# Projection with halves of heads as row tiles; values' bias later, sine products from PSUM, scale inside the exponential

## The reference

```
q, k, v = heads(x @ Wq.T + bq), heads(x @ Wk.T + bk), heads(x @ Wv.T + bv)
q, k = rope(q), rope(k)        # Y*cos + concat(-Y[8:], Y[:8])*sin
att  = softmax(where(causal, q @ k.T / 4, -inf));  y = (att @ v) @ Wo.T + bo
x    = layernorm(x + y)
h    = silu(x@w1.T*s1) * (x@w2.T*s2);  h = gelu(h@h1.T*hs1);  h = gelu(h@h2.T*hs2)
out  = layernorm(x + h@w3.T*s3)
```

## Time and profile before

| | us |
|---|---|
| median of three runs | 2792.42 (2791.34 to 2792.55) |
| the profiled execution's own time | 2795.36 |
| its span, first to last instruction | 2793.6 |
| projection stage, up to the first work of attention | 133.7 |
| all that follows | 2659.9 |

### The profile page before, as it was taken

How to read it: one execution, slowest core, us unless ns; L and a number is a source line. 1 busy time by engine, 2 the same in 40 slices (tenths; PEclk the granted TensorE clock), 3 DMA queues, 4 the chain that set the end, 5 groups by cost and what they waited for, 6 DMA issues and landing times.

```text
span 2793.6 us, 39368 instructions
## 1 busy us (share of the span) xinstructions
PE 2729.1 (98%) x14880; PEld 1424.9 (51%) x14880; DVE 1899.9 (68%) x4003; ACT 1348.4 (48%) x2641; POOL 138.3 (5%) x206
## 2 busy tenths in 40 slices
PE   8899999999999999999999999999999999999998
PEld 4423333333333333333323333588888887888887
DVE  6999999888888888888887774633333352443343
ACT  4436666777776777777777776411111111000100
POOL 3300110001100001100000000000000000000000
PEclk9979999999999999999999999999999999999999
DMA  7731110001110011110001000411111132121100
GB/s 217 204 74 39 30 30 26 3 15 32 29 43 6 5 33 32 30 34 3 1 3 39 19 5 9 118 58 58 58 58 58 43 128 108 46 82 54 45 16 23
DMA packets 95613, 133.47 MB, mean 48 GB/s; under 512 B 31462, under 2 KB 69094, under 8 KB 91718
## 3 DMA queue, kind: packets, MB, share of 16 engines
q1 hardware_dynamic: 81452, 96.25, 10.7%
q0 software_dynamic: 6336, 23.34, 3.8%
q10 hardware_dynamic: 7648, 11.54, 1.5%
HBM read 83.77 MB, written 47.32 MB: 47 GB/s over the span
## 4 chain that ended last, share of the span: by engine, by line
PE 88%; DVE 6%; issue 2%; ACT 1%; DMA 1%; SPq 0%; ACTq 0%; POOLq 0%; POOL 0%; DVEq 0%
PE wi_f L984 19%; PE at_o L533 18%; PE at_row L498 17%; PE at_key L512 16%; PE na_h L1202 13%; PE na_y L1214 3%; DVE at_segmax L584 3%; DVE fr_masked L580 1%; DMA values<-pr_vals 1%; ACT at_probs L648 1%; PE at_key L515 1%; PE wi_p L833 1%; DVE pr_parts L252 0%; DVE pr_full L248 0%; PE pr_main L130 0%
## 5 line engine op out<-in xcount | busy, mean ns | idle before, releaser
L648 ACT ACTIVATE at_probs<-at_key 128x512 f32<-128x512 f32 (+3 forms) x2304 | 1127.3, 567 | 502.4 <-PE at_key L512 353.2
L584 DVE TENSOR_REDUCE at_segmax<-at_row 128x1 f32<-128x512 f32 x1792 | 1142.8, 684 | 169.2 <-PE at_row L498 164.9
L512 PE MATMUL at_key<-fr_q_stack,fr_k_stack 99*128 99x512 bf16 (+3 forms) x1152 | 415.0, 365 | 1.3 <-ACT at_probs L648 1.0
L498 PE MATMUL at_row<-fr_k_stack,fr_q_stack 96*128 96x512 bf16 (+3 forms) x1152 | 404.6, 376 | 10.8 <-DVE at_mask L612 5.5
L498 PE MATMUL at_row<-at_k_stack,at_q_stack 96*128 96x512 bf16 (+3 forms) x1152 | 408.1, 364 | 1.8 <-DVE at_segmax L584 1.1
L512 PE MATMUL at_key<-at_q_stack,at_k_stack 99*128 99x512 bf16 (+3 forms) x1152 | 402.2, 364 | 7.5 <-ACT at_probs L648 6.9
L1202 PE MATMUL na_h<-fr_h,fr_h2w_h 128*128 128x512 f32 x1024 | 322.1, 396 | 1.4 <-DVE fr_h L730 1.4
L533 PE MATMUL at_o<-at_probs,fr_values 128*32 128x512 f32 (+3 forms) x2304 | 289.0, 574 | 0.0
L533 PE MATMUL at_o<-at_probs,at_values 128*32 128x512 f32 (+3 forms) x2304 | 287.9, 572 | 0.0
L580 DVE CUSTOM_DVE_ANT_0 fr_masked<-at_row,fr_causal 128x384 f32<-128x384 f32 (+3 forms) x512 | 243.8, 483 | 45.1 <-PE at_row L498 44.7
L498 PEld LDWEIGHTS at_row<-fr_k_stack,fr_q_stack 96*128 96x128 bf16 x1152 | 110.3, 99 | 308.3 <-DVE at_segmax L584 160.1
(11 more groups left out here) (121 smaller groups left out, 2558.1 us busy)
## 6 DMA issues: line engine op xcount, KB each, us to landing
hidden<-wi_h SPq DMA_DIRECT2D x64, 256.0 KB, 2.0
na_h2f<-hidden SPq DMA_DIRECT2D x8, 1024.0 KB, 7.7
q_parts<-pr_parts SPq DMA_DIRECT2D x48, 128.0 KB, 2.4
k_parts<-pr_parts SPq DMA_DIRECT2D x48, 128.0 KB, 3.3
at_q_stack<-q_parts POOLq DMA_DIRECT2D x48, 128.0 KB, 3.5
at_k_stack<-k_parts POOLq DMA_DIRECT2D x48, 128.0 KB, 3.8
values<-pr_vals SPq DMA_DIRECT2D x32, 136.0 KB, 3.3
outputs<-at_outs SPq DMA_DIRECT2D x128, 34.0 KB
```

Of the source, the lines that this page charges most:

```text
L498: last = nc.tensor.matmul(bank[:, 0:w], qst[u][0:SROWS, c, h, i * P:(i + 1) * P], kst[u][0:SROWS, h, s * CH:s * CH + w], start=True, stop= ...
L512: last = nc.tensor.matmul(bank[:, q0:CH], kst[u][0:SROWS + PARTS, h, j * P:(j + 1) * P], qst[u][0:SROWS + PARTS, c, h, q0:CH], start=True, ...
L584: nc.vector.tensor_reduce(segmax[:, n % 2, h * TPC + i, s:s + 1], row_ps[r % RING_R][:, 0:w], op=ALU.max, axis=AX.X).then_inc(rows_taken, 1)
L648: nc.scalar.activation(probs[:, g % RING_P, h, q0:CH], key_ps[m % RING_K][:, q0:CH], ACT.Exp).then_inc(probs_ready, 1)
```

## The change

Within `project` two units become one *pair*: 16 pairs, q and k of each chunk. The rows of the weights are reordered on the host, so that tile 0 holds the first halves of all 16 heads and tile 1 the second halves (`halves`). Then the rotation is an exchange of the two tiles: `full` half 0 = t1[0] - t2[1], half 1 = t1[1] + t2[0]. PE's `rotate`, its banks and `turn` go. DVE's sine product reads main's PSUM bank itself and adds the bias in the same instruction (`scalar_tensor_tensor`). hi, mid, rest and the third part go over both halves at once (1024 columns). SP stores each half with its three parts in one transfer (384 KB). ACT, not DVE, takes the values out of PSUM, without a bias. The bias of the values, which commutes with the softmax's weighted mean, is added to the outputs in `Prepare.scale`. The scale 1/4 goes into the exponential. `load_first` moves from ACT's queue to SP's; PE's waits for the constants and for the values move to where they are first needed. `parts` has 3 slots of pairs instead of 4 of units.

The diff, cut to the core:

```diff
@@ project, scalar
+            def take_values(n, i):
+                if n == 0:
+                    act.wait_ge(v_ones, 1)
+                else:
+                    act.wait_ge(v_stored[i], 32 * n)
+                act.wait_ge(v_ready, 2 * n + i + 1)
+                nc.scalar.activation(vals[:, i, :, :, 0:HD], v_ps[i][:, :, :].rearrange("p j (h d) -> p j h d", d=HD), ACT.Copy
+                                     ).then_inc(v_taken, 1)
...
             for g in range(NU + 1):
                 if g + 1 < NU:
                     linear(g + 1)
                 if g < NU:
-                    act.wait_ge(full_ready, g + 1)
+                    take_values(*divmod(g, PAIRS))
+                    act.wait_ge(full_ready, 2 * g + 2)
                     if g >= SLOTS:
-                        act.wait_ge(parts_stored[g % SLOTS], 16 * PARTS * (g // SLOTS))
-                    nc.scalar.activation(parts[:, g % SLOTS, 0, :], full[:, g % 2, :], ACT.Copy).then_inc(hi_ready, 1)
+                        act.wait_ge(parts_stored[g % SLOTS], 16 * 2 * (g // SLOTS))
+                    nc.scalar.activation(parts[:, g % SLOTS, 0, :, :], full[:, g % 2, :, :], ACT.Copy).then_inc(hi_ready, 1)
...
-                if 2 <= n < 2 + FIRST_EARLY:
...
-                    front.load_first(act, qp_d, kp_d, n - 2, range(m, len(TERMS), UNITS))
@@ project, vector
-                    dve.wait_ge(rot_ready, g + 1)
-                    nc.vector.tensor_tensor(t2[:, g % 2, :], rot_ps[g % 2][:, :], sin[:, n % BUFS, :], ALU.mult
-                                            ).then_inc(t2_ready, 1)
+                    for half in range(2):
+                        dve.wait_ge(lin_ready, 2 * g + half + 1)
+                        if g >= 1:
+                            dve.wait_ge(full_ready, 2 * (g - 1) + 2 - half)
+                        nc.vector.scalar_tensor_tensor(out=t2[:, half, :], in0=main_ps[2 * (g % 2) + half][:, :],
+                                                       scalar=bias[:, 2 * m + half:2 * m + half + 1], in1=sin[:, n % BUFS, :],
+                                                       op0=ALU.add, op1=ALU.mult).then_inc(t2_ready, 1)
...
-                if g < NU and m % 2 == 1:
...
-                    if n > 0:
-                        dve.wait_ge(v_stored[i], 32 * n)
-                    for j in range(2):
-                        last = nc.vector.tensor_tensor(
-                            vals[:, i, j, :, 0:HD], v_ps[i][:, j, :].rearrange("p (h d) -> p h d", d=HD),
-                            bv[:, :].rearrange("p (h d) -> p h d", d=HD), ALU.add)
@@ project, sync
+                early = n - 2
+                if 0 <= early < FIRST_EARLY:
...
+                    front.load_first(sp, qp_d, kp_d, early, range(m, len(TERMS), PAIRS))
                 sp.wait_ge(parts_ready, g + 1)
-                for a in range(PARTS):
-                    sp.dma_start((qp_d, kp_d)[m // DH][a, (m % DH) * P:(m % DH + 1) * P, n, :], parts[:, g % SLOTS, a, :]
-                                 ).then_inc(parts_stored[g % SLOTS], 16)
...
+                for half in range(2):
+                    sp.dma_start((qp_d, kp_d)[m].rearrange("a (p f) n t -> f p a n t", f=2)[half, :, :, n, :],
+                                 parts[:, g % SLOTS, :, half, :]).then_inc(parts_stored[g % SLOTS], 16)
+                sp.wait_ge(v_taken, g + 1)
+                for j in range(2):
+                    sp.dma_start(v_d[:, :, n, 2 * m + j, :].rearrange("q p e -> p q e"),
+                                 vals[:, m, j, :, :].rearrange("p (q h) e -> p q (h e)", q=NQUAD)
+                                 ).then_inc(v_stored[m], 16)
@@ attend, scalar
-                    nc.scalar.activation(probs[:, g % RING_P, h, q0:CH], key_ps[m % RING_K][:, q0:CH], ACT.Exp
+                    nc.scalar.activation(probs[:, g % RING_P, h, q0:CH], key_ps[m % RING_K][:, q0:CH], ACT.Exp, scale=HD ** -0.5
@@ Prepare.scale
         for a in range(DH):
             self.nc.vector.tensor_tensor(o[:, n % 2, a, :], o[:, n % 2, a, :], self.front.recip[:, :], ALU.mult
+                                         ).then_inc(self.scaled, 1)
+        for a in range(DH):
+            dve.wait_ge(self.scaled, DH * n + a + 1)
+            self.nc.vector.tensor_scalar(o[:, n % 2, a, :], o[:, n % 2, a, :], self.front.bv[:, a:a + 1], None, ALU.add
                                          ).then_inc(self.y_ready, 1)
```

More of the change, by code:

```diff
@@ L119, in main @@
             def main(g):
-                n, m = divmod(g, UNITS)
+                n, m = divmod(g, PAIRS)
                 if m == 0:
                     pe.wait_ge(x_loaded[n % BUFS], 16 * (n // BUFS + 1))
[L124 to L141, removed]
+                if n == 0:
+                    pe.wait_ge(w_loaded[m], 16)
+                for half in range(2):
+                    if g >= 2:
+                        pe.wait_ge(lin_ready, 2 * (g - 2) + half + 1)
+                        pe.wait_ge(t2_ready, 2 * (g - 2) + half + 1)
+                    bank = main_ps[2 * (g % 2) + half]
+                    for c in range(DH):
+                        last = nc.tensor.matmul(bank[:, :], w[m][:, c, half * P:(half + 1) * P], xt[:, n % BUFS, c, :],
+                                                start=(c == 0), stop=(c == DH - 1))
+                    last.then_inc(main_ready, 1)
             def values(n, i):
@@ L153, in values @@
                 last.then_inc(v_ready, 1)
-            main(0)
             for g in range(NU):
[L157 to L161, removed]
+                main(g)
+                values(*divmod(g, PAIRS))
         @block.scalar
         def _(act):
[L165 to L169, removed]
-            def linear(g):
[L173 to L179, removed]
+            def linear(g):
+                m = g % PAIRS
+                for half in range(2):
+                    act.wait_ge(main_ready, 2 * g + half + 1)
+                    if g >= 2:
+                        act.wait_ge(t1_ready, 2 * (g - 2) + half + 1)
+                    nc.scalar.activation(lin[:, g % 2, half, :], main_ps[2 * (g % 2) + half][:, :], ACT.Identity,
+                                         bias=bias[:, 2 * m + half:2 * m + half + 1]).then_inc(lin_ready, 1)
+            def take_values(n, i):
+                if n == 0:
+                    act.wait_ge(v_ones, 1)
[4 more added lines that the diff above has]
+                                     ).then_inc(v_taken, 1)
             load_weight(act, 0, "WqT")
@@ L814, in spread @@
         if n > 0:
-            queue.wait_ge(self.y_ready, DH * n)
+            queue.wait_ge(self.scaled, DH * n)
         for e in range(self.COPIES):
```

136 lines of the change are left out of this document (63 added, 73 removed).

## The result

The changed kernel takes 2869.35 us (median of 4 runs, 2867.56 to 2870.09), the kernel before 2791.88 beside it (4 runs, 2790.97 to 2792.55): ratio 1.0277 [1.0259, 1.0295]. Forecast was 2866, range 2828 to 2892. The profiled execution took 2867.56, its span is 2865.7.

The account below looks back on a forecast made before the run. PE bounds the span (98% busy), DVE the projection's pairs. A new closed loop, 12 x 13.2 + 10.7 = 169 us, puts the first maximum at 208: +74 on the 2792.4 median gives 2866 us, range 2828 to 2892.

Parts of the forecast that it names:

- The loop: Projection: ACT's taking of values, ahead of `hi`, waits for the store of pair g-2; 13.2 us per pair, chance 0.60.
- Length of a turn: Projection, per pair: 7.2 us from `hi` to parts' end, 5.4 to the values' landing, 0.6 for taking them.
- The meeting of POOL and DVE: Projection: POOL's products hold up DVE's full and parts; a pair takes 13.2 us, 10.7 without the meeting.
- The store's term: Projection: from parts' end to the values' landing 5.4 us; last issue starts 1.4 behind, bounds 4.35 and 13.
- The estimate from the Trainium skill: Four transfers after the parts: about 2.0 us fixed plus bytes at 436 GB/s, landing some 4.4 us after them.
- The loads in five of twelve turns: ACT's three loads ahead of linear: POOL's meeting avoided, 2.5 us less, against about 2.8 us more; left at 13.2.
- Start and end: Projection: third `hi` at 33.5 us, last turn 10.7, last `hi` at 202.6, first maximum at 208; shift +74.
- What is hidden: Values' bias at most 11 us if exposed, taken as nothing; first loads on SP covered; wait for `parts_stored` nothing.
- The numbers I gave for single rows: Profile after: ACT waits 6 to 8 us for the values' DMA, 14 times; PE busy 83 of 208 us.
- the shorter loop: Rival: POOL and DVE miss each other or the landing hides extra bytes; 10.7 per pair, +44, 2836 us; chance 0.24.
- No change: Rival: no loop, but POOL always against DVE's operations with two SBUF inputs; 7.3 per pair, 2789 us; chance 0.04.
- faster: Rival: the store lands so early that `hi` never waits; 6.0 per pair, 2770 us; chance 0.05.

Follow-up runs that it names:

- 2: Changed kernel with four value buffers instead of two, every queue's order as it was: 2785.93 us, ratio 0.9975 to the kernel before.
- 1: Changed kernel with SP storing the values ahead of its wait for the parts: 2800.16 us, ratio 1.0029 to the kernel before.
- 3: Changed kernel with the values' two stores issued ahead of the parts' stores, still behind the wait for the parts: 2840.09 us.
- 4: Changed kernel with a pair's parts stored in six transfers of 128 KB instead of two of 384 KB: 2878.82 us.
- 5: Changed kernel with both products on DVE, none on POOL, and no linear tiles on ACT: 2840.37 us.
- 10: Kernel before, with ACT taking the values ahead of `hi` in place of DVE, values' bias left out: 2797.58 us, ratio 1.0016.
- 11: Changed kernel with DVE, not ACT, taking the values at the end of its iteration: 2868.43 us.
- 12: Changed kernel with DVE taking the values, and loads of x issued once the pair before has its values taken: 2846.07 us.
- 8: Changed kernel with four value buffers, four slots of `parts` and both products on DVE: 2775.86 us, ratio 0.9938 to the kernel before.
- 9: Changed kernel with four value buffers, four slots, both products on DVE, and the values' store ahead of the wait for parts: 2773.25 us, ratio 0.9934.

## Why the prediction was right, point by point

- **The loop** was read rightly: taking the values waits for a store that stands behind the parts of the pair two before. Shown by 2 (with more buffers the slowdown is gone), 1 (with the store issued earlier nearly so), 3 to 5 (each part of the turn shortened or lengthened moves the time by about thirteen times that).
- **What closes it** was told only in part. I laid the weight on ACT's order ("stands ahead of `hi`"). Runs 10 to 12 show that ACT's place is the smaller half: ACT ahead of `hi` in units costs 6 us at the first maximum, and DVE's own place in pairs costs 77 us (11), or 54 when the loads of x are out of the way (12). What closes the loop is that one iteration is now a pair: the store of two pairs ago is issued behind the parts of the very iteration in which the buffer is asked for. In the kernel before these parts were done two iterations of a unit earlier: the store is issued at 119.86, and DVE asks for the buffer at 125.09, 5.2 us later (I had called this a whole pair, 6.67).
- **Length of a turn:** 7.2 + 5.4 + 0.6 = 13.2 forecast, 6.7 + 6.35 + 0.5 = 13.56 at 102.5 us, 13.32 on average. Two errors cancel in part, and that 2866 came within 4 us of 2869 is to this extent luck.
  - The meeting of POOL and DVE was forecast at 2.5, run 5 gives 2.15.
  - The store's term was too small by 0.95 in this turn. The last issue starts 1.76 behind the parts' end (110.98) where I had 1.4, since the values' two issues take 1.83 us behind 384 KB transfers and not 1.06; from there to the landing 4.6 passed where I took 4.0.
  - The estimate from the Trainium skill (DMA: Bandwidth & Descriptors, Anatomy of one DMA) of 4.4 from the parts is farther off; the measured 6.35, or 5.8 in the calmer turn, decides.
  - Half a us of the landing goes with something that I overlooked: the loads of the stacks, issued right behind the values' stores (from 112.15 on). In the eight landings without them the last issue's start is followed by the landing after 4.0 to 4.3 us, in the six with them after 4.4 to 5.0. A turn without them, in which 5.8 us pass from the parts' end (162.69) to the landing:

```profile
163.73 1.82 SPq L270 DMA_DIRECT2D values<-pr_vals  x2
...
168.50 0.60 ACT L170 ACTIVATE pr_vals<-pr_v 128x512 f32<-128x512 f32 x1 [9.37 <-DMA values<-pr_vals]
```

- **The loads in five of twelve turns:** I let 2.5 less for POOL and 2.8 more for the bytes cancel out. Neither was there: at 102.22 the loads are issued 7 us ahead of the stores, POOL meets DVE as always (3.06 for two products), and the five turns with loads (13.41 on average) are nearly as long as the seven without (13.26). My 2.8 us is right where loads and stores do meet (run 11, 2.6 to 3.7 us).
- **Start and end:** third `hi` forecast at 33.5, was 35.33, since POOL met the first parts too (2.29 at 26.51) and the store took 0.7 longer; last turn 10.7 and 11.03; last `hi` 202.6 and 206.22; first maximum 208 and 211.06. Shift +74 forecast, +77 measured.
- **What is hidden:** the values' bias costs nothing that can be measured: from the last exponential to the end 1020.7 us in both profiles. ACT does not wait for `parts_stored`. Both as forecast. The issues of `load_first` lie in SP's wait, as forecast, but the traces speak against its transfers being free: the six of the twelve turns that have them last 13.60 us on average, the six others 13.05, some 3 us in all. Runs 5 and 12 show the same (11.64 against 10.86 in run 5). No run takes these loads out, and whether they would cost as much from ACT's queue was not tested.
- **From the first maximum to the end "as before within 5 us":** 2654.6 against 2659.5. The 5 us lie between the first and the last exponential (1608.6 against 1614.7). Windows of 40 us, 24 us behind the first exponential, of the changed kernel and then of the kernel before:

```profile
260.40:300.40 40.00, 37.48 (x233) 12.36 (x229) 38.74 (x92) 24.62 (x49) 4.18 (x8) 1.00 0.26 53
```

```profile
182.20:222.20 40.00, 37.89 (x209) 11.94 (x208) 35.08 (x83) 21.41 (x43) 3.14 (x6) 0.87 0.29 47
```

  In the fourteen profiles of this case, whose attention differs in no more than the exponential's scale, that distance lies between 1607.3 and 1615.2 us; with a clock of 0.87 or 0.96 in this window it is 1607.3 to 1615.2, with 1.00 1608.0 to 1613.2. So it is a spread of single executions or of the start, not a gain of the change; the clock alone does not explain it, and its cause stays open.
- **The numbers I gave for single rows:** ACT's wait 6 to 8 us, 14 times: it is 9.4, 14 times. That one did not follow from my own sum, in which 13.2 less ACT's 3.6 of work leaves 9.6. PE was to be busy for 83 us; it is 114, because the lower clock that I had allowed for came (0.78; the values' matmuls take 1.89 us more in the turn shown), and PE is still not in the loop.
- **The rivals:** the shorter loop fell because POOL does meet DVE in every turn. "No change" and "faster" had the right sizes for a loop that is open: with four buffers the kernel takes 2786, without POOL's products and with four slots 2776.

## What to carry to other kernels

When iterations are merged into larger ones, count for each buffer how many iterations lie between the issue of the store that frees it and the next writing, in instructions of each queue, not in data: here the two value buffers stayed two, and what had been issued two iterations ahead of the asking came to be issued in the same iteration, behind it. A store that stands in one queue behind another wait belongs to the loop, so try first a third and fourth buffer, and only then the order. In a loop with a DMA inside, also ask which other transfers are issued in the microsecond ahead of it: here loads of x placed there cost 2.6 to 3.7 us each time, and nothing 5 us earlier; with loads placed right behind the stores, turns were half a us longer.

## What the runs showed of the hardware that I had not expected

- The two issues of the values' store (136 KB each) on SP's queue take 0.93 us together when they stand first, 1.07 behind six transfers of 128 KB and 1.83 behind two of 384 KB. Why was not tested.
- A DVE operation of 1024 columns is held up for about as long as one of 512: 1226 ns alone, 2206 with POOL's product in the way (0.98 us more), 512 columns in the earlier trace rows 1.08 more.
- With 0.5 of the DMA engines' time used, transfers in a chain still set the pace; with 0.95 to 1.1 used, removing two thirds of ACT's wait gained nothing that the intervals show (8 against 9).
